# Second attention of a four-block transformer step: scores of eight heads in one round, the norm before it spread into its loop, two shared steps moved ahead of the experts

## The reference, cut to what matters

```python
def _L0_ffn_ref(hidden_states, w_router, gate_up_proj, down_proj, w_gate, w_up, w_down):
    logits = x @ w_router.T                       # 16 experts, TOP_K = 1
    ...
    expert_out = jnp.einsum('etf,efh->eth', up * jax.nn.silu(gate), down_proj)
    shared = jax.nn.silu(x @ w_gate.T) * (x @ w_up.T) @ w_down.T
    out = shared + expert_out.sum(axis=0)

def _L1_xattn_ref(query, key, value, Wq, bq, Wk, bk, Wv, bv, Wo, bo):
    HEADS, HEAD_DIM = 16, 16
    q = query @ Wq.T + bq; k = key @ Wk.T + bk; v = value @ Wv.T + bv
    scores = jnp.einsum('bhqd,bhkd->bhqk', q, k) * scale
    probs = jax.nn.softmax(scores, axis=-1)
    out = jnp.einsum('bhqk,bhkd->bhqd', probs, v)
    return out @ Wo.T + bo

x = x + _L0_xattn_ref(ctx_1024, _layernorm(x), ...)
x = x + _L0_ffn_ref(_layernorm(x), ...)
x = x + _L1_xattn_ref(_layernorm(x), ctx_1024, ctx_1024, ...)
x = x + _L1_ffn_ref(_layernorm(x), ...)
```

## Time and profile before

| | before |
|---|---|
| median of 3 runs | 1633.43 us (1629.73 to 1634.49) |
| the profiled execution | 1631.14 us, of which the span is 1629.4 us |
| PE busy | 1458.9 us, 90% |
| DVE busy | 942.6 us, 58% |
| ACT busy | 874.4 us, 54% |
| POOL busy | 638.8 us, 39% |
| mean granted TensorE clock | 0.953 |

### The profile page before, as it was taken

The page is one execution under the profiler, slowest core; times in us unless marked ns, Lnnn a source line. Parts: engine busy times, 40 slices in busy tenths (PEclk is TensorE's granted clock), DMA queues, the critical chain, the costliest instruction groups (busy, mean ns, idle before and its releaser), DMA issues. The chain is left out here.

```text
span 1629.4 us, 28395 instructions
## 1 busy us (share of the span) xinstructions
PE 1458.9 (90%) x9884; PEld 1193.4 (73%) x9884; DVE 942.6 (58%) x1777; ACT 874.4 (54%) x2184; POOL 638.8 (39%) x886
## 2 busy tenths in 40 slices
PE   4999999999999999877999994799998539999995
PEld 4878887878787888666888883466564528888885
DVE  5776767666767676655311116577877554444442
ACT  3886868677868686624211113566664214444442
POOL 6514444434444430323200015332231025787875
PEclk9999999999999999988999997899999559999998
DMA  4400000000000000012699963000000313455442
GB/s 137 164 1 21 1 21 2 21 3 20 2 14 8 1 1 1 1 33 83 220 314 312 317 210 52 26 8 14 8 1 1 127 61 110 124 121 123 120 123 27
DMA packets 74448, 120.27 MB, mean 74 GB/s; under 512 B 7008, under 2 KB 55136, under 8 KB 74304
## 3 DMA queue, kind: packets, MB, share of 16 engines
q1 hardware_dynamic: 63600, 101.76, 19.4%
q0 software_dynamic: 10704, 16.65, 5.1%
HBM read 99.78 MB, written 18.61 MB: 73 GB/s over the span
## 5 line engine op out<-in xcount | busy, mean ns | idle before, releaser
L508 ACT ACTIVATE a_p<-a_s,a_negmax 128x512 f32<-128x512 f32 x256 | 176.2, 688 | 111.6 <-DVE a_negmax L632 61.4
L632 DVE TENSOR_REDUCE a_negmax<-a_s 128x1 f32<-128x512 f32 x256 | 176.5, 689 | 76.6 <-PE a_s L371 72.7
L273 POOL TENSOR_TENSOR a_o_l<-a_o,a_o_h 128x256 fp32r<-128x256 f32 x64 | 46.9, 735 | 299.5 <-ACT a_o_h L533 299.5
L1561 ACT ACTIVATE h_probs<-h_scores,h_negmax 128x256 f32<-128x256 f32 x256 | 118.0, 475 | 81.7 <-DVE h_negmax L1728 81.7
L380 PEld LDWEIGHTS a_t<-ident,a_p 128*128 128x128 f32 x1024 | 122.5, 141 | 51.3 <-issue 21.6
L380 PE MATMUL a_t<-ident,a_p 128*128 128x128 f32 x1024 | 157.1, 276 | 0.7 <-DVE a_pT L647 0.7
L1973 POOL TENSOR_TENSOR n_w_l<-n_raw,n_w_h 128x768 fp32r<-128x768 f32 x64 | 118.2, 1847 | 75.3 <-ACT n_w_h L2016 75.3
L398 PE MATMUL a_out_p<-a_pT,a_v 128*64 128x256 f32 x1024 | 124.6, 385 | 0.0
L370 PE MATMUL a_s<-a_k_hl,a_q_hh 128*128 128x512 f32 x256 | 106.4, 415 | 2.6 <-issue 1.9
L1728 DVE TENSOR_REDUCE h_negmax<-h_scores 128x4 f32<-128x1024 f32 x64 | 78.0, 1221 | 49.4 <-PE h_scores L1655 49.4
L1666 PEld LDWEIGHTS h_turned<-ident,h_probs 128*128 128x128 f32 x512 | 54.7, 141 | 64.7 <-issue 45.8
(11 more groups left out here) (357 smaller groups left out, 4382.1 us busy)
## 6 DMA issues: line engine op xcount, KB each, us to landing
e_w_in<-in_L_ffn_gate_up_proj SPq DMA_DIRECT2D x31, 1024.0 KB, 7.1
n_raw<-in_L_ffn_w SPq DMA_DIRECT2D x64, 384.0 KB, 3.1
e_w_out<-in_L_ffn_down_proj SPq DMA_DIRECT2D x31, 512.0 KB, 5.4
rows_in<-a_zeros SPq DMA_DIRECT2D x1, 3968.0 KB, 15.3
e_rows<-rows_in SPq DMA_DIRECT2D x31, 128.0 KB, 5.3
rows_out<-e_result POOLq DMA_DIRECT2D x31, 128.0 KB, 4.6
a_both<-in_ctx SPq DMA_DIRECT2D x8, 256.0 KB, 2.7
a_both<-in_x SPq DMA_DIRECT2D x8, 256.0 KB, 3.0
```

The costliest lines, as they stand in the source:

```text
L508: act.activation(probs[j][:, :], scores[j % 2][:, :], ACT.Exp, bias=negmax[:, j:j + 1], accum_out=total[:, r % 2, j % 2, j // 2:j // 2 + 1 ...
L632: dve.tensor_reduce(negmax[:, j:j + 1], scores[j % 2][:, :], AX.X, ALU.max, negate=True).then_inc(max_set, 1)
L1561: ins = act.activation(probs[s % 4][:, j, :], scores[s % 2][:, j // 2, j % 2, :], ACT.Exp, bias=negmax[:, s % 4, j:j + 1], accum_out=total ...
```

## The change

It has three parts.

1. Early steps. `EARLY` now counts steps: 14 of the 16 shared steps run ahead of the experts. In VectorE's list `add` stands ahead of the routing part of the same step, and routing parts 1 to 4 stand in steps 3 to 6 (before: 3, 4, 4, 5). ScalarE weights the 16 row tiles in three steps (5, 5 and 6 tiles) in place of four.
2. The norm. At the end of the mixture only group 0 (batches 0 and 1) is normalised, inside the last shared step, and only 8 of the 16 gathers run there. Group 1 is normalised by VectorE at the start of the attention. Batches 4 to 7 are gathered by GpSimd one batch at a time in the attention loop; VectorE finds their moments (`measure`), GpSimd the root and the product (`normalise`). In batch b the loop transposes batch b + 1 (`turn_x`, in the bank `proj`) and writes its high and low parts (`high_x`, `low_x`).
3. The scores. A round replaces two steps: four matmuls on all four 32-row tiles of the array make eight heads by 128 queries and fill both score buffers. A round's `score` waits for all exponentials of the round before.

```diff
-    EARLY = 3
+    EARLY = 14
...
-                sp.wait_ge(hidden_set, FC * EARLY - 2)
+                sp.wait_ge(hidden_set, EARLY - 2)
                 load_weights(1)
...
-                for t in range(NT):
-                    if t < TILES * EARLY:
-                        pool.wait_ge(added, t // TILES + 1)
+                for t in range(2 * TILES):
+                    pool.wait_ge(added, t // TILES + 1)
                     pool.indirect_dma_start(g.x[:, t, :], None, g.rows_out[:, :],
...
@@ TensorE, end of the mixture
-                for b in range(NB):
+                for b in range(2):
                     turn_sums(b)
+                down(FC * GROUPS - 1)
...
@@ ScalarE, end of the mixture
+                    if n == FC * GROUPS - 1:
+                        apply(0)
+                        apply(1)
                     silu_of(n)
                     high_of(n)
-                apply(0)
-                apply(1)
-                for b in range(NB):
+                for b in range(2):
                     high_x(b)
-                    if b + 2 < NB:
-                        apply(b + 2)
...
@@ VectorE, end of the mixture
-                for n in range(FC * EARLY, FC * GROUPS):
+                for n in range(EARLY, FC * GROUPS):
+                    if n == FC * GROUPS - 1:
+                        normalise(0)
                     shared(n)
...
@@ GpSimd, attention
+                def normalise(b):
+                    rows, xn, mv = g.x[:, 2 * b:2 * b + 2, :], g.xn[:, 2 * b:2 * b + 2, :], l_mv[b % 2]
+                    pool.wait_ge(x_measured, b - LATER + 1)
+                    link(pool.tensor_tensor(xn, rows, along(mv[:, :, 0]), ALU.subtract))
...
++                    pool.tensor_tensor(xn, xn, along(p_rstd[:, :]), ALU.mult).then_inc(x_later, 1)
...
                     add_bias(b)
                     spread_inverse(b, 0)
+                    if b + LATER < NB:
+                        normalise(b + LATER)
                     if b + 2 < NB:
                         low_ctx(b + 2)
                     low_o(b, 0)
+                    if b + LATER + 1 < NB:
+                        gather(b + LATER + 1)
...
@@ TensorE, attention
-                    wait(pe, exp_set, n - 1)
-                    for j in range(2):
-                        at = s // 2 % 2 * 2 * PAD + j * PAD
-                        rows = slice(at, at + PAD)
-                        ins = pe.matmul(scores[s % 2][:, j, :, :], q[b % 2][rows, m, half * P:(half + 1) * P],
+                    wait(pe, exp_set, 2 * n)
+                    for j in range(FOUR):
+                        rows = slice(j * PAD, (j + 1) * PAD)
+                        ins = pe.matmul(scores[j // 2][:, j % 2, :, :], q[b % 2][rows, m, half * P:(half + 1) * P],
                                         kz[b % 2][rows, m, :, :], start=True, stop=True)
-                    ins.then_inc(scored, 1)
+                        if j % 2:
+                            ins.then_inc(scored, 1)
...
+                    for i in range(ROUNDS):
+                        score(b, i)
+                        if i == 0 and b and b + 1 < NB:
+                            turn_x(b + 1)
+                        if i:
+                            turn(b, 2 * i - 2)
+                        elif b:
+                            turn(b - 1, STEPS - 2)
+                        if i == 1 and b:
+                            weigh(b - 1, 1)
+                        if i == 1 and b + 1 < NB:
+                            project_q(b + 1)
+                        if i == 2 and b:
+                            project_out(b - 1)
+                        if i == 3:
+                            weigh(b, 0)
+                        if i == 3 and b + 1 < NB:
+                            project_v(b + 1)
+                        if i:
+                            turn(b, 2 * i - 1)
+                        elif b:
+                            turn(b - 1, STEPS - 1)
+                        if i == 0 and b + 1 < NB:
+                            project_k(b + 1)
```

More of the change, by code:

```diff
@@ L958, in _ @@
                                             compute_op=ALU.add).then_inc(routed[t // TILES], 16)
-                for grp in range(GROUPS):
+                for grp in range(2):
                     pool.wait_ge(routed[grp], 16 * TILES)
@@ L1077, in _ @@
                 turn_x(1)
-                for n in range(FC * EARLY):
+                for n in range(EARLY):
                     shared(n, 0)
@@ L1081, in _ @@
                         count()
-                down(FC * EARLY - 1)
+                down(EARLY - 1)
                 pe.wait_ge(row_set, 1)
@@ L1377, in _ @@
                 apply(3)
[L1378 removed]
+                for n in range(EARLY):
                     shared(n)
[L1380 to L1386 removed]
+                    if n % FC == 0 and n:
+                        add(n // FC - 1)
+                    if n in range(3, 7):
+                        route(n - 2)
                     elif n == 8:
                         scale_queries()
[L1389 to L1391 removed]
+                if EARLY % FC == 0:
+                    add(EARLY // FC - 1)
                 set_rowsT(0)
@@ L1515, in _ @@
                 low_ctx(1)
+                gather(LATER)
                 for b in range(NB):
@@ L1619, in project_q, with turn_x @@
                     ins.then_inc(q_done, 1)
+                def turn_x(b):
+                    if b < LATER:
+                        pe.wait_ge(x_normed, b - FIRST + 1)
+                    else:
+                        pe.wait_ge(x_later, b - LATER + 1)
+                    pe.wait_ge(v_set, b)
+                    for kc in range(KC):
+                        for t in range(2):
+                            ins = pe.transpose(proj[:, kc, t * P:(t + 1) * P], g.xn[:, 2 * b + t, kc * P:(kc + 1) * P], g.ident[:, :])
+                    ins.then_inc(x_turned, 1)
                 def project_v(b):
@@ L1759, in add, with measure @@
                     dve.tensor_tensor(rows, rows, proj[:, :, :], ALU.add).then_inc(added, 1)
+                def measure(b, part):
+                    if part == 0:
+                        dve.wait_ge(routed[b], 32)
+                        for t in range(2):
+                            ins = dve.bn_stats(l_stats[:, t, :], g.x[:, 2 * b + t, :])
+                        ins.then_inc(l_chain, 1)
+                    else:
+                        dve.wait_ge(l_chain, b - LATER + 1)
+                        wait(dve, x_later, b - LATER - 1)
+                        for t in range(2):
+                            ins = dve.bn_aggr(l_mv[b % 2][:, t, :], l_stats[:, t, :])
+                        ins.then_inc(x_measured, 1)
```

202 lines of the change are left out of this document (116 added, 86 removed).

## The result

| | before | after |
|---|---|---|
| median (lowest to highest) of 16 runs each, us | 1634.06 (1628.85 to 1640.09) | 1628.26 (1618.21 to 1635.04) |
| ratio after / before, 95% interval | | 0.9961 (0.9944 to 0.9979) |
| the profiled execution: time, span | 1631.14, 1629.4 | 1629.72, 1628.0 |
| granted clock, mean over the span | 0.953 | 0.942 |

The changed kernel is faster by 0.4%, some 6 us, where 1618 had been forecast for a kernel at 1631. Cut at the same five places, the two profiled executions read as follows.

A forecast was written before the change was run, and what follows sets the result against it. TensorE was taken to bound the attention, a chain of small steps the stretch before it. Norm -20.6, rounds 0, clock +10 and early steps -2.5 gave -13.1 on 1631.14: 1618 us, range 1604 to 1634.

The forecast's parts named there:

- The norm, 20.6 us: Between experts and attention: first shared product to the attention's first transfer falls from 48.7 to 28.1 us, saving 20.6.
- 0.2 us for `project_k` in round 0: Attention loop: in the first round of six batches `project_k` waits for `low_x`, holding the next scores back by 0.2 us.
- The rounds, 0: Attention loop: 32 rounds of 6.72 us plus tails make 222.3 us against 222.4 before, so no gain.
- Four row tiles side by side: Attention scores: four matmuls on four row tiles run together in 1.13 us; two pairs in turn would take 2.26.
- The clock, +10: Attention loop: TensorE's clock falls behind gaps in rounds with little work for it, costing 10 us; bounds 0 and 25.
- the price of a fall: Attention loop: each fall of TensorE's clock costs 1.5 us.
- in 7 of some 10 places: Attention loop: the number of rounds with gaps at which the clock was taken to fall.
- the clock falls in most rounds: Rival: clock falls in most attention rounds, or tails are half a microsecond longer per round; 1628 to 1643 us, chance 0.15.
- my own case: Main forecast for the whole kernel: clock falls at some places, 1618 us, own range 1612 to 1627, chance 0.47.
- The early steps, -2.5: Before the experts: two steps moved ahead cost 8.3 us, shorter waits and less half clock give it back; net -2.5.
- If the 2.85 us gap stays, the net is 0; if it goes too, -4.6: Early part: net effect in us, depending on whether a 2.85 us gap goes along with its slow stretch.
- at about 775 against 776: Early part: the 16 scatters end at about 775 us against 776, the weighting on ScalarE being done a step sooner.

The follow-up runs named there:

- e8: e1 with the turned norm rows in the contexts' bank and no filling in round 0 of the middle batches: 1607.58 us, ratio to before 0.9851.
- e1: The changed kernel with unread TensorE transposes filling rounds 0 and 2 of middle batches and the first and last batch: 1613.82 us, ratio to before 0.9889.
- e6: The changed kernel with half of e1's filling transposes in the same places (4 and 6 in a middle batch): 1613.78 us, ratio to before 0.9882.
- e5: The changed kernel with e1's filling in round 2 of each batch alone: 1614.82 us, ratio to before 0.9886.
- e9: The kernel before with the new order of VectorE's early work alone, still twelve early steps: 1633.08 us, ratio to before 1.0014.
- e10: The changed kernel with ten filling transposes per batch in the busy rounds (4 in round 1, 6 in round 3): 1632.99 us, ratio to before 1.0031.
- e11: e8 with twelve early steps instead of fourteen: 1606.45 us, ratio to before 0.9856.
- e13: The changed kernel with twelve early steps instead of fourteen and nothing else: 1622.81 us, ratio to before 0.9956.
- e15: e11 with GpSimd's four subtractions one behind each of the first four expert blocks: 1598.80 us, ratio to before 0.9806.
- e14: e1 with GpSimd's four subtractions one behind each of the first four expert blocks: 1608.01 us, ratio to before 0.9863.
- e12: e8 with eleven early steps, so five shared steps stand after the experts: 1605.11 us, ratio to before 0.9851.
- e16: e12 with GpSimd's four subtractions one behind each of the first four expert blocks: 1601.52 us, ratio to before 0.9820.
- e4: The kernel before with the attention's four rounds a batch alone, norm and early steps as before: 1634.34 us, ratio to before 1.0021.
- e7: e1 with twelve early steps instead of fourteen: 1607.27 us, ratio to before 0.9843.

## Why the prediction was off

**The norm, 20.6 us: right**, each link of the chain included; the down product, taken at 2.8 us for half the clock, ran from 996.11 to 999.03 at a granted clock of 0.50. What the prediction left out is the norm's price inside the loop. It had 0.2 us for `project_k` in round 0; undisturbed batches show 0.8 us in all in rounds (27.54 to 28.3) in batches 1 to 3 and 0.5 in batches 4 to 6 (27.98 to 28.01), which measure no moments; more than half of the 0.8 is that very wait (e8).

**The rounds, 0: right for the two together.** A plain round was 6.72 in the forecast and 6.75 to 6.84 measured (e1); the loop with the clock held at all but its first rounds is 223.4 to 223.8 us (e6, e1) against 222.3. That the gain is nothing comes from terms of opposite sign that the forecast did not separate: in a middle batch -1.2 for the rounds and +0.8 or +0.5 for the norm, together some -3 over six batches, and +4 in the first and last batch (27.04 and 26.15 for 24.24 and 24.77).

**Four row tiles side by side: right**, 1.14 us for 1.13.

**The clock, +10: the step that failed by its size.** That falls come behind the gaps was right, and so was the price of a fall. The granted clock is at 0.50 in twelve stretches of the changed kernel's loop, and in one of e1's besides the one that ends as its loop begins: 16.5 us (240.3 less 223.8) for eleven falls, 1.5 each, as taken. The step that failed is the number, "in 7 of some 10 places". The ten gaps of over 2 us that I had counted are there (2.38 to 3.48 us; round 2 of each batch, and the first round of the first and the last), and nine of them, not seven, brought a fall; batch 1's did not. Three more falls came in round 0 of batches 3, 5 and 6, behind gaps of at most 1.12 us, which I had not counted at all. Each of these three followed a fall in the batch before, and with round 2 filled (e5) only one was left; but that one had no fall in the 78 us before it, so that one fall makes the next likelier is a guess. In number the outcome, 1628.26, is that of the rival "the clock falls in most rounds", 1628 to 1643, at its lower edge, and just outside my own case (1612 to 1627); the rival's condition did not come true, for a fall came in twelve stretches of 32 rounds. It took the early steps as well to get there.

**The early steps, -2.5: no gain**, and the second cause of the miss: +1.4 in the profiled pair, +2.1 counted from the mixture's own start, +0.9 on average over the eight traces of this early code. The step that failed is "If the 2.85 us gap stays, the net is 0; if it goes too, -4.6". I priced what the waits gave back, and not what the new order would bring together. I also had the 16 scatters end "at about 775 against 776"; they ended at 777.63 against 775.79, since the later routing starts them 4.5 us later. GpSimd's four subtractions then run back to back, and in e9, e10, e11 and e13 VectorE's subtraction of two SBUF tiles ends 0.55 us behind the last of them, after 5.9 to 6.0 us for 0.69. That was worth 0.5% in e11 (e15), but the changed kernel's own trace does not have this row; what held its last early steps is open (below). Before the experts two steps cost 5.2 us (e14 against e15); behind them four steps are hidden under gathers and norm (28.2 us with two steps, e14, and with four, e15), five are not (31.2, e12 and e16). Twelve early steps are better than fourteen by the traces (e15 against e14); between twelve and eleven the runs do not decide.

By the runs, then: -20.6 for the norm, +16.5 for the clock, +1.4 for the early part, +1.2 before the first scores, +1.4 in the loop's own length, -1.3 behind it, together -1.4 in the profiled pair. What lies between this and the 5.8 us of the medians is within the scatter of single runs, which goes with the clock: over the 28 runs of the kernel before that stand beside e1 to e4, times from 1626.86 to 1645.28 us go with mean granted clocks from 0.957 down to 0.944.

**What stays open.** Why rounds and norm together bring the clock down so much more often (0.89) than the rounds alone (0.97), was not taken apart: TensorE idles in a batch for 4.9 us in the one (27.54 less 22.68) and for 4.8 in the other (28.36 less 23.61), both have a gap of 2.4 us in round 2, and what differs is the batch's length and the place of the shorter gaps. And the cause of the waits of 4.50 and 3.20 us in the changed kernel is not known. That they had the same cause as the 5.93 us row could only be argued from their absence in e14, and their times speak against it: the wait of 4.50 ended at 774.72, and GpSimd's first subtraction began at 777.66, so it can't have been behind the subtractions; for the 3.20 us, which ended at 779.79, it stays possible. Besides, in e1 and e14 the first shared product comes at the same time (969.12 and 969.33), though e14's scatters began 2 us later.

## What to carry to other kernels

This stage was limited by a chain through three engines and left TensorE gaps (2.38 to 2.44 us in round 2). Such a gap itself cost nothing (28.36 us in batch 1 of the changed kernel, 28.32 with filling, both at clock 1.00), but the clock fell behind seven of these eight and slowed the work on the chain (1.5 us a fall): look at the granted clock of the rounds, and where it falls, try a microsecond of idle work in the emptiest rounds (ratio 0.9882, e6), not anywhere (1.0031, e10). Before work is moved ahead of a stage to fill a wait, ask where it is hidden now; here up to four steps were free behind the experts (28.2 us with two and with four, e14 and e15), and two cost 5.2 us before them. And when an order is changed, list what each queue will now run back to back, on GpSimd against VectorE above all (5.93 us for 0.69 in e11).

## What the runs showed of the hardware

- The granted clock fell from 1.00 to 0.50 behind nine of ten gaps of 2.38 us or more in a loop in which TensorE is busy for 82% of the time (197.86 of 240.28 us), and ten transposes per middle batch, started 0.11 us apart, in the two thin rounds, kept it at 1.00 (e6), where five of the six middle batches of the changed kernel have a stretch at 0.50; in the busy rounds the same ten left seven falls of eight (e10). The gap and the busy share do not decide alone: in e4 five batches in a row, each with a gap of 2.38 or 2.39 us and TensorE busy for 82% (113.41 of 137.75 us), stayed at clock 1.00.
- A VectorE subtraction with both inputs in SBUF took 5.93 us instead of 0.69 while GpSimd ran four SBUF subtractions back to back (e11). VectorE's product of a PSUM and an SBUF tile took its 0.69 us beside the same GpSimd work (e7: 778.76, with GpSimd busy from 776.09 to 779.83). The long record lasts over all four instructions of GpSimd: it begins 0.46 us ahead of the first (775.84 and 776.30) and ends 0.55 us behind the last. And it does not always come: of the thirteen traces that have the subtractions there, behind the new order, four have the row.
- Four matmuls on four row tiles take 1.14 us, in eight records, the time that two on two tiles took the earlier trace rows.
